# Cross-attention and feed-forward: GpSimd's feed-forward additions in 512-column pieces, the biases on another wait

## The chip, the cores and the metric

The kernel runs on 1 core of one Trainium2 chip. The metric is device time in microseconds (us) of one execution. TensorE (PE in the profile) multiplies, VectorE (DVE), ScalarE (ACT) and GpSimd (POOL) work element by element, SyncE (SP) issues DMAs. The engines run their own instruction lists in order and meet at semaphores.

## The reference, cut to what matters

```python
x = x + xattn(layernorm(x), ctx)          # x: 8 x 1024 x 512, 16 heads, 64 keys
h   = layernorm(x) @ W1 + b1              # 512 -> 2048
im  = w_imag * sin(theta + 0.1 * h)
q   = h + (cos(theta)*w_real + sin(theta)*w_imag) * im * 0.1
x   = x + relu(q) @ W2 + b2               # 2048 -> 512
```

All is float32. The kernel writes every matmul as three, over a high and a low part of each operand (`product`, lines 1983 to 1985), so that splitting into `hi` (ScalarE) and `lo = full - hi` (VectorE) accounts for much of the element work.

## The kernel before, in words

The 8192 rows are 16 tiles of 512 rows (`TILES`), held as 4 blocks (`NB`) of 128 partitions x 512 channels. Up to about 625 us the attention part runs, tile by tile; it is not touched. The rest is the feed-forward part.

Its first two tiles ("the plain part", about 640 to 812 us) go chunk by chunk: 16 chunks of 128 hidden channels for each tile. TensorE makes a chunk of hidden values, ScalarE and VectorE make sin and relu of it, TensorE multiplies it with W2 three chunks later. The other 14 tiles go in pairs, in seven phases T = 1 to 7. In a phase, the first matmul is a Strassen scheme: 8 steps p = 0 to 7, and in each seven products P1, P6, P4, P2, P5, P7, P3 (this order) give four 128 x 512 hidden blocks, two for each tile (i = 8(T-1) + p counts the steps through). After P7, before P3, come the W2 multiplications of two chunks ("seconds") of the pair's first tile. After step 7 come the last two seconds of the first tile and then those of the second tile, c = 0, 1, 2, ...; no new hidden work is made in that stretch, and the operands of the next phase are prepared in it.

What the engines do in a step, in the order of their lists:

- VectorE: `hidden_12` of the step before (L1829), `wave(2)` (L1848), `sum_u` (L1797), `positive_lo` (L1855), `fraction(3)` (L1834), `wave(3)`, `fraction(0)`, then the step's sums `sum_v` (L1805, waits for P7), `hidden_21` (L1814) and `hidden_22` (L1822, the last of them, counts up `c22_done`), then `wave(0)`, in some steps statistics or transposes for later tiles, `fraction(1)`, `fraction(2)`, `positive_lo`, `wave(1)`.
- `fraction` reads frac and turns, `wave` frac and the hidden block, `positive_lo` the hidden block and act_hi: two operands in SBUF each. So do `operand_lo` (L1783), `split_lo` (L1565) and `sum_to_lo` (L1789). The step's sums and `add_outputs` (L1867) have one operand in PSUM; transposes (L1560) and statistics (L1517) have one operand.
- TensorE waits in `strassen`: P5 of the next step for `hidden_12` (`c12_done`), P7 for `sum_u`, P3 for `hidden_22` (`c22_done`); in `second(e)` for `positive_lo` of that chunk, and, where a new output is begun, for `add_outputs` of the output before.
- GpSimd: `add_row_bias` (L904) adds bo to two of the four blocks of a coming tile's rows, `add_last_bias` (L913) adds b2 + bo to two blocks of the residual that the output is added to, `operand_sums` (L1130) makes the Strassen differences T1, T2, T4, T3 of the next phase, one after the other, when `add_outputs` of the first tile is done. `rsqrt` (L881) and `add_parts` (L535, on 256 columns) are smaller.

In a phase before the last, `add_row_bias` is called four times: in step 0 for the first half on P1 and for the second half on P7 of that step, then on P7 of step 1 and on P7 of step 2; `add_last_bias` for the first tile once in step 6 and once in step 7, on their P7. In phase 7 there are only the last biases. The one for the second tile follows `operand_sums` or, in phase 7, follows at once.

```python
for half in range(2):                                   # p = 0 and p = 1
    pool.wait_ge(prod, at_prod(i + (p if half else 0), "P7") - (NP - 2) * (p + half == 0))
    add_row_bias(2 * T + 2 + p, half)
```

Of the kernel before, what the change touches and what calls it, by code (L numbers as in the profile page):

```python
# [11 lines left out]
ALU = mybir.AluOpType  # L12
# [3 lines left out]
P = 128  # L16
BANKS, BANK = 8, 512
B, N, C = 8, 1024, 512
# [10 lines left out]
NB = TOK // P  # L29
# [15 lines left out]
NP = len(PRODUCTS)  # L45
# [107 lines left out]
def xattn_ffn(nc, x, ctxt, wq, bq, wk, bk, wv, bv, wo, bo, w1, b1, phases, w_real, w_imag,  # L153
# [6 lines left out]
    with stack:  # L160
# [32 lines left out]
        bo_row = sbuf(stack, "bo_row", [P, C])  # L193
# [118 lines left out]
        x1_whole = sem("x1_whole")  # L312
# [158 lines left out]
        def at_prod(i, name):  # L471
            return NP * i + PRODUCTS.index(name) + 1
# [389 lines left out]
        def _(pool):  # L862
# [37 lines left out]
            def add_row_bias(T, half):  # L900
                blocks = slice(half * NB // 2, (half + 1) * NB // 2)
                pool.wait_ge(x_in[T % 2], x_loads(TILES + T))
                rows = x_sb[T % 2][:, blocks, :]
                pool.tensor_tensor(rows, rows, bo_row[:].unsqueeze(1).to_broadcast([P, NB // 2, C]), ALU.add)\  # L904
                    .then_inc(x1_whole, 1)

            def add_last_bias(T, half):
                blocks = slice(half * NB // 2, (half + 1) * NB // 2)
                pool.wait_ge(acc_in[T % 2], 16 * (T // 2 + 1))
                if T == 0:  # L910
                    pool.wait_ge(b2_biased, 1)
                rows = acc[:, T % 2, blocks, :]
                pool.tensor_tensor(rows, rows, b2_row[:].unsqueeze(1).to_broadcast([P, NB // 2, C]), ALU.add)\  # L913
                    .then_inc(acc_biased, 1)

            rsqrt(0)

# [200 lines left out]
            def operand_sums(T, names):  # L1118

                for name in names:  # L1120
                    j = OPERAND_SUMS.index(name)
                    if name == "T1":
                        for half in range(2):
                            pool.wait_ge(a_back[half], 16 * (turned_at(2 * T + 1) + 1))
                    else:
                        pool.wait_ge(t_done, 4 * (T - 1) + j)
                    if name == "T4":
                        pool.wait_ge(xo_lo_done, NP * (T - 1) + OPERANDS.index("B21") + 1)
                    a, b = {"T1": ("B12", "B11"), "T2": ("B22", "T1"), "T4": ("T2", "B21"), "T3": ("B22", "B12")}[name]
                    pool.tensor_tensor(PLACE[name], PLACE[a], PLACE[b], ALU.subtract).then_inc(t_done, 1)  # L1130

            for j in range(FC + HALF1 + 4):
                pool.wait_ge(turns_done, j + 1)
# [21 lines left out]
            for T in range(1, FFN_PAIRS):  # L1155
                more = T + 1 < FFN_PAIRS
                for p in range(FP):
                    i = (T - 1) * FP + p
                    if more and p < 2:
                        for half in range(2):  # L1160
                            pool.wait_ge(prod, at_prod(i + (p if half else 0), "P7") - (NP - 2) * (p + half == 0))
                            add_row_bias(2 * T + 2 + p, half)
                    if more and p == 2:
                        rsqrt(TILES + 2 * T + 2)
                    if more and p == 4:
                        rsqrt(TILES + 2 * T + 3)
                    if p >= FP - 2:
                        pool.wait_ge(prod, at_prod(i, "P7"))
                        add_last_bias(2 * T, p - FP + 2)
                if more:  # L1170
                    pool.wait_ge(y2_done, NB * (2 * T + 1))
                    operand_sums(T + 1, OPERAND_SUMS)
                for half in range(2):
                    add_last_bias(2 * T + 1, half)
# [1092 lines left out]
```

## Time and profile before

| | |
|---|---|
| median of 3 runs | 2005.63 us (2000.49 to 2009.94) |
| the profiled execution | 2007.17 us, its span 2005.4 us |
| PE busy | 1957.9 us (98%) |
| VectorE busy | 1605.7 us (80%) |
| ScalarE busy | 1261.5 us (63%) |
| GpSimd busy | 749.9 us (37%) |
| mean granted TensorE clock | 0.995 of full speed |

The span runs from the first to the last instruction; 1.8 us of the execution lie around it. Start times are us from the span's start. In the rows, L is the line of the kernel; in timeline rows the number in square brackets is the time that the engine stood idle before the instruction, and what ended it; "x2" is two instructions merged in one row, with the time from the start of the first to the end of the last. An instruction's recorded time holds also what it waited for after it was issued.

### The profile page before, as it was taken

How to read it: one execution, taken by the hardware profiler on the slowest of the kernel's cores; microseconds unless marked ns; L12 is line 12 of the kernel's file. 1: busy time of each engine (PE TensorE's matmuls, PEld its weight loads, DVE VectorE, ACT ScalarE, POOL GpSimd, SP SyncE). 2: the span in 40 equal slices, each digit the busy share in tenths (PEclk: the TensorE clock that was granted, in tenths of full speed). 3: DMA queues.
4: the chain of work that ended last, by engine and by line, in shares of the span. 5: the costliest groups of instructions: out<-in, count | busy, mean ns of one | idle time of the engine just before them, and what ended most of it. 6: DMA issues, size and time to landing. Idle time of an engine off the chain costs nothing.

```text
span 2005.4 us, 27939 instructions
## 1 busy us (share of the span) xinstructions
PE 1957.9 (98%) x9162; PEld 1625.9 (81%) x9162; DVE 1605.7 (80%) x2272; ACT 1261.5 (63%) x2132; POOL 749.9 (37%) x453
## 2 busy tenths in 40 slices
PE   9999999999999999999999999999999999999999
PEld 7788888888887788787887788788778878878877
DVE  8988888888876987888688778968878886886773
ACT  6767767666655876676477467546736755754661
POOL 6877777777774533202311320311131032031020
PEclk9999999999999999999999999999999999999999
DMA  7465664665536998787778688777877877876645
GB/s 245 149 164 140 171 170 129 174 177 152 157 100 209 315 338 269 263 247 235 263 242 251 223 265 258 244 261 235 237 259 244 253 240 253 257 235 228 225 138 189
DMA packets 347459, 441.29 MB, mean 220 GB/s; under 512 B 165552, under 2 KB 201392, under 8 KB 347312
## 3 DMA queue, kind: packets, MB, share of 16 engines
q1 hardware_dynamic: 346448, 439.44, 70.7%
q8 instruction: 75, 1.23, 0.2%
q14 instruction: 72, 0.59, 0.1%
q10 hardware_dynamic: 864, 0.04, 0.0%
HBM read 347.90 MB, written 91.23 MB: 219 GB/s over the span
## 4 chain that ended last, share of the span: by engine, by line
PE 56%; DVE 22%; ACT 11%; issue 9%; POOL 1%; DVEq 0%; DMA 0%; ACTq 0%; POOLq 0%
PE psum L1983 18%; PE psum L1985 17%; PE psum L1984 17%; DVE frac L1834 4%; ACT turns L1408 3%; DVE act_lo L1855 3%; DVE hid L1848 3%; PE psum L2076 2%; ACT frac L1384 2%; DVE acc L1867 2%; DVE stats L1517 2%; ACT x_sb L1208 2%; ACT act_hi L1436 1%; DVE late_hid L1848 1%; DVE late_hid L1805 1%
## 5 line engine op out<-in xcount | busy, mean ns | idle before, releaser
L1983 PE MATMUL psum<-w_ring,act_hi 128*128 128x512 f32 x1024 | 403.7, 394 | 27.2 <-DVE act_lo L1855 26.1
L1985 PE MATMUL psum<-w_ring,act_lo 128*128 128x512 f32 x1024 | 402.1, 393 | 0.0
L1984 PE MATMUL psum<-w_ring,act_hi 128*128 128x512 f32 x1024 | 402.0, 393 | 0.0
L1983 PE MATMUL psum<-xo,w_ring 128*128 128x512 f32 x784 | 307.6, 392 | 6.0 <-DVE late_hid L1822 3.6
L1985 PE MATMUL psum<-xo,w_ring 128*128 128x512 f32 x784 | 305.8, 390 | 0.0
L1984 PE MATMUL psum<-xo,w_ring 128*128 128x512 f32 x784 | 305.6, 390 | 0.0
L1834 DVE SCALAR_TENSOR_TENSOR frac<-frac,turns 128x512 f32<-128x512 f32 x256 | 223.5, 884 | 68.9 <-ACT frac L1384 68.0
L1983 PEld LDWEIGHTS psum<-w_ring,act_hi 128*128 128x128 f32 x1024 | 194.1, 190 | 73.9 <-issue 33.7
L1421 ACT ACTIVATE frac<-frac 128x512 f32<-128x512 f32 x256 | 156.4, 627 | 151.6 <-DVE frac L1834 151.6
L1985 PEld LDWEIGHTS psum<-w_ring,act_lo 128*128 128x128 f32 x1024 | 194.1, 190 | 40.8
L1984 PEld LDWEIGHTS psum<-w_ring,act_hi 128*128 128x128 f32 x1024 | 194.4, 190 | 40.0
L913 POOL TENSOR_TENSOR acc<-acc,b_row 128x1024 f32<-128x1024 f32 x32 | 85.5, 2684 | 330.6 <-PE psum L1985 330.6
L1384 ACT ACTIVATE frac<-turns,round_col 128x512 f32<-128x512 f32 x256 | 185.3, 724 | 13.4 <-DVE hid L1848 6.2
L904 POOL TENSOR_TENSOR x_sb<-x_sb,bo_row 128x1024 f32<-128x1024 f32 x30 | 76.3, 2552 | 290.0 <-DMA x_sb<-x_dram 150.9
L1983 PEld LDWEIGHTS psum<-xo,w_ring 128*128 128x128 f32 x784 | 147.2, 188 | 46.0 <-issue 15.4
L1985 PEld LDWEIGHTS psum<-xo,w_ring 128*128 128x128 f32 x784 | 147.2, 188 | 30.8
L1984 PEld LDWEIGHTS psum<-xo,w_ring 128*128 128x128 f32 x784 | 147.3, 188 | 29.4
L1436 ACT ACTIVATE act_hi<-late_hid 128x512 fp32r<-128x512 f32 x112 | 70.0, 630 | 158.2 <-PE psum L1985 158.2
L1855 DVE SCALAR_TENSOR_TENSOR act_lo<-late_hid,act_hi 128x512 fp32r<-128x512 f32 x112 | 127.0, 1155 | 42.7 <-ACT act_hi L1436 42.7
L970 POOL TENSOR_TENSOR prob<-prob,top 128x1024 f32<-128x1024 f32 x64 | 122.0, 1906 | 72.8 <-DVE top L1653 72.7
L949 POOL TENSOR_TENSOR prob<-prob,inv 128x1024 f32<-128x1024 f32 x64 | 123.4, 1928 | 42.2 <-DVE inv L1635 42.1
L1848 DVE SCALAR_TENSOR_TENSOR hid<-frac,gain,hid 128x512 f32<-128x512 f32 x134 | 116.3, 868 | 26.9 <-ACT frac L1421 26.9
(187 smaller groups left out, 4420.5 us busy)
## 6 DMA issues: line engine op xcount, KB each, us to landing
w_ring<-w2s SPq DMA_DIRECT2D x240, 512.0 KB, 4.1
w_ring<-w1s SPq DMA_DIRECT2D x392, 256.0 KB, 3.6
x_sb<-turn_dram SPq DMA_DIRECT2D x58, 512.0 KB, 6.0
res<-in_x SPq DMA_DIRECT2D x64, 256.0 KB, 3.6
x_dram<-res SPq DMA_DIRECT2D x64, 256.0 KB, 3.1
acc<-x_dram SPq DMA_DIRECT2D x16, 1024.0 KB, 8.1
x_sb<-in_x SPq DMA_DIRECT2D x15, 1024.0 KB, 6.3
x_sb<-x_dram SPq DMA_DIRECT2D x15, 1024.0 KB, 7.9
```

Of the source, the lines that this page charges most:

```text
L913: pool.tensor_tensor(rows, rows, b2_row[:].unsqueeze(1).to_broadcast([P, NB // 2, C]), ALU.add)\
L949: pool.tensor_tensor(rows, rows, inv[:, (i - 1) % 2, :].unsqueeze(2) .to_broadcast([P, NB * HG, KEYS]), ALU.mult).then_inc(prob_done, 1)
L970: pool.tensor_tensor(rows, rows, top[:, i % 2, :].unsqueeze(2).to_broadcast([P, NB * HG, KEYS]), ALU.subtract).then_inc(shift_done, 1)
L1384: act.activation(frac[:, q % 2, :], turns[:, q % 2, :], ACT.Identity, bias=round_col[:]).then_inc(whole_done, 1)
L1421: act.activation(frac[:, q % 2, :], frac[:, q % 2, :], ACT.Sin, scale=-SIN_SCALE).then_inc(sin_done, 1)
L1436: act.activation(act_hi[:, e % ACTS, :], source, ACT.Relu).then_inc(act_hi_done, 1)
L1834: dve.scalar_tensor_tensor(out=frac[:, q % 2, :], in0=frac[:, q % 2, :], scalar=ROUND, in1=turns[:, q % 2, :], op0=ALU.subtract, op1=ALU.s ...
L1848: dve.scalar_tensor_tensor(out=rows, in0=frac[:, q % 2, :], scalar=gain[:, f:f + 1], in1=rows, op0=ALU.mult, op1=ALU.add).then_inc(wave_do ...
L1855: dve.scalar_tensor_tensor(out=act_lo[:, e % ACTS, :], in0=rows, scalar=0.0, in1=act_hi[:, e % ACTS, :].bitcast(F32), op0=ALU.max, op1=ALU ...
L1983: pe.matmul(o, a_hi, b_hi, start=first, stop=False, skip_group_check=resumed)
L1984: pe.matmul(o, a_hi, b_lo, start=False, stop=False, skip_group_check=resumed)
L1985: return pe.matmul(o, a_lo, b_hi, start=False, stop=last, skip_group_check=resumed)
```

## The change

Three edits, all in GpSimd's list. Both bias helpers go over their two blocks one by one: two additions of 512 columns take the place of one of 1024. Each operand sum is made in two instructions of 512 columns. And the biases of the phases wait for `c22_done` of a step where they waited for one of its products. Only the last piece of each group counts up the semaphore, as the one instruction did. The biases of the plain part keep their place in the list.

```diff
             def add_row_bias(T, half):
                 blocks = slice(half * NB // 2, (half + 1) * NB // 2)
                 pool.wait_ge(x_in[T % 2], x_loads(TILES + T))
-                rows = x_sb[T % 2][:, blocks, :]
-                pool.tensor_tensor(rows, rows, bo_row[:].unsqueeze(1).to_broadcast([P, NB // 2, C]), ALU.add)\
-                    .then_inc(x1_whole, 1)
+                for n in range(blocks.start, blocks.stop):
+                    row = x_sb[T % 2][:, n, :]
+                    last = pool.tensor_tensor(row, row, bo_row[:], ALU.add)
+                last.then_inc(x1_whole, 1)
 
             def add_last_bias(T, half):
...
-                rows = acc[:, T % 2, blocks, :]
-                pool.tensor_tensor(rows, rows, b2_row[:].unsqueeze(1).to_broadcast([P, NB // 2, C]), ALU.add)\
-                    .then_inc(acc_biased, 1)
+                for n in range(blocks.start, blocks.stop):
+                    row = acc[:, T % 2, n, :]
+                    last = pool.tensor_tensor(row, row, b2_row[:], ALU.add)
+                last.then_inc(acc_biased, 1)
...
-                    pool.tensor_tensor(PLACE[name], PLACE[a], PLACE[b], ALU.subtract).then_inc(t_done, 1)
+                    for rows in (slice(0, NB // 2), slice(NB // 2, NB)):
+                        last = pool.tensor_tensor(PLACE[name][:, rows], PLACE[a][:, rows], PLACE[b][:, rows], ALU.subtract)
+                    last.then_inc(t_done, 1)
...
                         for half in range(2):
-                            pool.wait_ge(prod, at_prod(i + (p if half else 0), "P7") - (NP - 2) * (p + half == 0))
+                            pool.wait_ge(c22_done, i + 1 + (p if half else 0))
                             add_row_bias(2 * T + 2 + p, half)
...
                     if p >= FP - 2:
-                        pool.wait_ge(prod, at_prod(i, "P7"))
+                        pool.wait_ge(c22_done, i + 1)
                         add_last_bias(2 * T, p - FP + 2)
```

## Rows read from the trace of the kernel before

**Rows 1.** The page, part 1: busy time and share of the span.
```profile
PE 1957.9 (98%) x9162; PEld 1625.9 (81%) x9162; DVE 1605.7 (80%) x2272; ACT 1261.5 (63%) x2132; POOL 749.9 (37%) x453
```
**Rows 2.** PE's waits: who, for whom, us in total, times, longest.
```profile
PE psum L1983 <- DVE act_lo L1855: 26.1, 14, 2.6
PE psum L1983 <- DVE late_hid L1822: 3.6, 7, 0.6
PE psum L1983 <- ACT p_sb L1391: 1.9, 1, 1.9
PE psum L1983 <- DVE acc L1867: 1.1, 1, 1.1
```
**Rows 3.** PE's timeline: idle times in phases 1, 3 and 7.
```profile
915.22 0.47 PE L1983 MATMUL psum<-xo,w_ring 128*128 128x512 f32 x1 [0.53 <-DVE late_hid L1822]
933.83 0.47 PE L1983 MATMUL psum<-w_ring,act_hi 128*128 128x512 f32 x1 [1.86 <-DVE act_lo L1855]
948.31 0.47 PE L1983 MATMUL psum<-w_ring,act_hi 128*128 128x512 f32 x1 [1.69 <-DVE act_lo L1855]
...
1274.77 0.47 PE L1983 MATMUL psum<-w_ring,act_hi 128*128 128x512 f32 x1 [1.85 <-DVE act_lo L1855]
1287.61 0.47 PE L1983 MATMUL psum<-w_ring,act_hi 128*128 128x512 f32 x1 [1.69 <-DVE act_lo L1855]
...
1951.17 0.47 PE L1983 MATMUL psum<-w_ring,act_hi 128*128 128x512 f32 x1 [2.57 <-DVE act_lo L1855]
```
**Rows 4.** Windows (stretch; length; busy of PE to POOL; clock; DMA), behind idle times.
```profile
933.80:937.20 3.40, 3.37 (x11) 2.71 (x12) 3.15 (x6) 2.69 (x5) 0.00 (x0) 0.69 0.41 160
...
1274.80:1278.20 3.40, 3.40 (x15) 2.83 (x16) 3.15 (x6) 2.63 (x5) 0.00 (x0) 1.00 0.44 171
```
**Rows 5.** By line: duration in ns, min/median/max, of GpSimd's 1024- and 512-column instructions.
```profile
L913 POOL TENSOR_TENSOR acc<-acc,b_row x32: 2388/2838/2959, 696.8 to 1947.1; 128x1024 f32<-128x1024 f32 x32
...
L891 POOL TENSOR_TENSOR q_lo<-q_full,q_hi x61: 1287/1295/1879, 29.2 to 596.6; 128x512 fp32r<-128x512 f32 x61
```
**Rows 6.** GpSimd's timeline: steps 7 of phases 1 and 7, the first operand sum.
```profile
925.09 2.39 POOL L913 TENSOR_TENSOR acc<-acc,b_row 128x1024 f32<-128x1024 f32 x1 [13.35 <-PE psum L1985]
942.05 2.78 POOL L1130 TENSOR_TENSOR temps<-x_sb 128x1024 f32<-128x1024 f32 x1 [14.57 <-DVE acc L1867]
...
1941.88 7.99 POOL L913 TENSOR_TENSOR acc<-acc,b_row 128x1024 f32<-128x1024 f32 x3 [12.55 <-PE psum L1985]
```
**Rows 7.** VectorE's timeline beside GpSimd's 1024- and 256-column instructions in the plain part.
```profile
788.04 2.88 DVE L1848 SCALAR_TENSOR_TENSOR hid<-frac,gain,hid 128x512 f32<-128x512 f32 x1
...
665.04 1.23 DVE L1834 SCALAR_TENSOR_TENSOR frac<-frac,turns 128x512 f32<-128x512 f32 x1
```
**Rows 8.** VectorE's timeline: steps 6 and 7 of phase 1.
```profile
909.41 2.88 DVE L1848 SCALAR_TENSOR_TENSOR late_hid<-frac,gain,late_hid 128x512 f32<-128x512 f32 x1 [0.70 <-ACT frac L1421]
...
925.38 2.66 DVE L1834 SCALAR_TENSOR_TENSOR frac<-frac,turns 128x512 f32<-128x512 f32 x1 [0.58 <-ACT frac L1384]
...
929.52 0.69 DVE L1822 TENSOR_TENSOR late_hid<-psum,late_hid 128x512 f32<-128x512 f32 x1
...
933.00 0.68 DVE L1855 SCALAR_TENSOR_TENSOR act_lo<-hid,act_hi 128x512 fp32r<-128x512 f32 x1
```
**Rows 9.** VectorE's timeline behind phase 1's first output.
```profile
942.49 2.89 DVE L1848 SCALAR_TENSOR_TENSOR late_hid<-frac,gain,late_hid 128x512 f32<-128x512 f32 x1
945.30 3.46 DVE L1855 SCALAR_TENSOR_TENSOR act_lo<-late_hid,act_hi 128x512 fp32r<-128x512 f32 x2
```
**Rows 10.** Timelines, step 0 of phase 1: two GpSimd instructions back to back, VectorE beside them.
```profile
820.33 5.21 POOL L904 TENSOR_TENSOR x_sb<-x_sb,bo_row 128x1024 f32<-128x1024 f32 x2 [21.55 <-DMA x_sb<-x_dram]
...
820.44 2.84 DVE L1848 SCALAR_TENSOR_TENSOR hid<-frac,gain,hid 128x512 f32<-128x512 f32 x1
```
**Rows 11.** Timelines, phase 2: `hidden_12` of step 0, first matmul of step 1's P5.
```profile
996.84 0.68 DVE L1829 TENSOR_TENSOR late_hid<-psum,late_hid 128x512 f32<-128x512 f32 x1
...
1001.47 0.39 PE L1983 MATMUL psum<-xo,w_ring 128*128 128x512 f32 x1
```

## The prediction

> **What bounds the kernel now.** I read the page first: TensorE is busy for 1957.9 of 2005.4 us [rows 1], so a gain can only come from its idle times and its clock. The list of PE's waits names the idle times: 26.1 us in 14 waits for `positive_lo`'s low part (L1855), 3.6 in seven for `hidden_22` (L1822), and one each for ScalarE's P1 copy and for an output sum [rows 2]; all of them lie in the feed-forward part. The timeline of PE then gives their places. A phase has three: A, 0.53 us (P3 of step 6 waits for `hidden_22`); B, 1.86 us behind step 7 (the last seconds wait for `positive_lo`); C, 1.70 us, 14 us later, in the seconds of the second tile [rows 3]. They return in phases 1 to 6 with the same sizes; phase 7 has one B of 2.57 us. The plain part has 1.94 (at 668), 1.07 (at 736) and 1.93 us (at 813), and phase 1 one more of 0.58 at 839.
>
> Five of the idle times are followed by a stretch at the lower clock (1.2 GHz for 2.4): windows behind B read 0.69 in phase 1 and 1.00 in phase 3 [rows 4]. Of six B of 1.86 us three were followed by such a stretch, of six C of 1.70 none, and the 1.94 and the 2.57 were. Its price: from B to C it takes 948.31 - 933.83 = 14.48 us with it and 1287.61 - 1274.77 = 12.84 without [rows 3], so about 1.65 us.
>
> Next, why VectorE is late. Its instructions with two operands in SBUF take about 0.7 us, but 2.66 to 2.9 when a 1024-column GpSimd instruction runs, and end about 0.6 us after that one ends [rows 6 to 9]. Sums with a PSUM operand, transposes and statistics keep their 0.69 us (the `hidden_22` row of [rows 8] is one of them). So GpSimd holds something that the two-operand instructions need, one engine at a time. The Trainium skill ("SBUF — State Buffer", on the two separate sides) says this too: a shared port pair, held for a whole instruction by whichever engine starts first. The trace agrees.
>
> **How long a piece holds it.** Where both engines have work without pause they alternate: in the plain part VectorE's instructions take 2.88 us beside 1024-column ones and 1.23 beside 256-column ones [rows 7]; consecutive ones overlap by about 0.08, so a round is 2.81 and 1.15. With 0.6 us of VectorE's own, the hold is 2.2 us for 1024 columns and 0.55 for 256. A line between them gives 1.1 us for 512. Alone, 512 columns take 1.29 us and 1024 take 2.39 [rows 5], so a pair of pieces is 0.2 us longer than one instruction. The bounds: below, half of 2.2; above, 1.88 us, the longest contested 512-column instruction [rows 5], less the 0.6 it waited, 1.3. I take 1.1. The new operand pattern (a plain row where a repeated one was) is seen in no row at 1024 columns; `q_lo` of [rows 5] has a plain one.
>
> **Does VectorE get in between two pieces?** At 820.33 two GpSimd instructions ran back to back without a wait between them, and VectorE's, issued at 820.44, ended at 823.28, after the first and 2.3 us before the end of the second at 825.54 [rows 10]. So it does. The Trainium skill speaks for a doubt ("GPSIMD Engine Reference", Instruction dispatch): consecutive GpSimd instructions are no barrier, each of the cores begins the next when its own share is done. By that alone a pair of pieces might hold the pair of ports without a gap, and splitting would give nothing; the sum would then be 1997 us, the third rival below, which is worked out from rows. The trace speaks against it here.
>
> **C goes.** When `add_outputs` ends, T1 is issued at 942.05 [rows 6]. Before, `wave(3)` waited for all of it (to 945.38), and the next `positive_lo` for all of T2, to 948.15 [rows 9]; PE had been ready at 946.62. After: piece one holds to 943.6, `wave(3)` ends 944.2, piece two 945.3; act_hi is there at 944.6, so `positive_lo` ends at 945.95, 0.7 before PE needs it. The next has to be done at 946.62 + 2.72 = 949.34 (one second is twelve matmuls at 0.227) and ends about 948.7. Later ones had more slack with holds of 2.2. Six times 1.70: 10.2 us.
>
> **A and B, the moved wait.** Before, the bias of step 6 was issued at P7 and held up `wave` at 909.41 by 2.14 us, the bias of step 7 (925.09) `fraction(0)` at 925.38 by 1.97 [rows 6, 8], both ahead of the step's three sums, which need no shared port. After, nothing holds these; `hidden_22` of step 6 comes about 1.45 us earlier (it is then held by ScalarE's part of the chain), and A is gone. But each bias now meets `wave(0)`, `fraction(1)`, `fraction(2)` and `positive_lo`. In step 7, `hidden_22` ends 1.97 earlier, at 928.24; `wave(0)` goes first, piece one holds 928.85 to 930.0, `fraction(1)` ends 930.6, piece two 931.8, `fraction(2)` 932.45, `positive_lo` 933.05 where it ended 933.68 [rows 8]. So 0.6 us are won of the 2, the rest is given back behind the sums. PE comes 0.53 earlier, since A is gone, while VectorE's chain, late from the bias of step 6, comes only about 0.2 earlier: B is then about 1.55. A and B together: 2.39 less 1.55, 0.85 us, six times 5.1 us. In phase 7 the last three biases are issued together, at 1941.88 before [rows 6], the first hidden wholly by the sums, and two (4.4 us) ahead of `fraction(1)` and `(2)`. After, six pieces from 1944.7 on: three are ahead of `positive_lo`, which ends 1949.8 for 1951.03; B falls to about 1.35, and about 0.5 us come with the pieces behind it. 0.7 us.
>
> **Step 0 to 2.** Both halves of step 0 now stand behind one wait, so four pieces follow each other, from 992.2 in phase 2. They put `wave(0)`, two fractions, `positive_lo` and `wave(1)` 4.4 us apart; `hidden_12` then ends at 999.7 for 997.5, and P5 needs it at 1001.47 [rows 11]: 1.8 us of slack. The delay reaches `fraction(3)` (1.3 us late) and `fraction(0)` of step 1, but that one was held up by a bias before and is no more, so `hidden_22` of step 1 comes at 1009.5, against 1009.73 before and 1009.87 when P3 needs it. Steps 1 and 2: two pieces behind the sums in place of one hold before them, with about 1 us of slack at P5 and P7. Costed at nothing, with this thin cover.
>
> **Plain part.** At 736 a 1024-column hold stands before `add_outputs`; half of it goes: 1.07 us. From 782 to 799 six GpSimd instructions hold VectorE to one instruction in 2.8 us; at 1.7 its backlog (ScalarE's turn at 804.66, which at 5.44 us a chunk was due at 802.2) goes, and with it the 1.93 at 813. At 668 VectorE has work without pause, so the same port time mostly stays: 0.6. At 839 0.3. Together 3.9 us.
>
> **Clock.** All idle times that stay are under 1.70 us, behind which no row has half clock: five stretches of 1.65, 8.2 us.
>
> **Sum.** 10.2 + 5.1 + 0.7 + 3.9 + 8.2 = 28.1 us. The profiled execution took 2007.17 us (span 2005.4), 1.5 more than the median of 2005.63; 2005.6 - 28.1 is 1978 us. No new queue and no DMA is added: the biases issue none, and nothing behind them in GpSimd's list (`rsqrt`, due a step later) is pushed past its time.
>
> **Rivals.**
> 1. The clock does not come back (0.17): B of 1.55 is near 1.70, and what would still be followed by half clock is open. 1978 + 8.2: 1986 us.
> 2. Step 0's four pieces are too many (0.11). If a piece holds 1.6 us rather than 1.1, `hidden_12` comes 0.2 after P5's time and `hidden_22` of step 1 about 1.5 late, six times: 9 us back, 1987. For: the cover of 0.4 at P3. Against: [rows 7].
> 3. No hand-over between pieces (0.08). C, the 736 and the 813 stay, phase 7 gets 2.2 worse, A and B still win 5.1, and three clock stretches go (5.0): 8 us, 1997. Against: [rows 10].
> 4. Slower (0.06): a piece holds the ports nearly as long as 1024 columns did, as if the hold were a cost of the instruction. At 2.2 us, step 0 makes `hidden_22` of step 1 4 us late (24 us in six phases), B grows by 2.2 (13 us) and C stays: about 2043. It decides from about 1.85 us a piece on, where the losses of step 0, B and C (36 us for each us of hold) eat the 28. Against: the 256-column round of 1.15 us.
>
> **Numbers.** My forecast has 0.58. Its own range is 1969 (B gone as well, 9 us more) to 1985. With rivals 1 and 2 that reaches to 1994; rivals 3 and 4 stay outside. 0.5%, 10 us, is about what this measurement tells from no change. Faster: 0.58 + 0.17 + 0.11 = 0.86. Same: rival 3, 0.08. Slower: rival 4, 0.06.
>
> **What would show it.** In the changed profile: no idle PE at C; VectorE's contested instructions at 1.7 to 1.8 us, none at 2.9; `wave` before the sums of steps 6 and 7 at 0.75; B at 1.3 to 1.6 with clock 1.00 behind it; no new wait for `late_hid` in step 1. Wrong, if PE waits there, or if B is above 1.86: then the sums were the better cover.

## The result: 1975.08 us, 1.5% faster, and the profile after

The changed kernel takes 1975.08 us (median of 4 runs, 1974.92 to 1976.86); the kernel before, run beside it, 2005.97 (4 runs, 2000.49 to 2009.94). The ratio is 0.985 (0.9826 to 0.9874). The prediction said 1978 in 1969 to 1994. The profiled execution took 1974.92 us, its span is 1973.1 and its granted clock 1.0; against the span of the profile of before that is 32.3 us less.

The page after, part 1 (to be read beside [rows 1]):
```profile
PE 1944.6 (99%) x9162; PEld 1620.7 (82%) x9162; DVE 1597.4 (81%) x2272; ACT 1264.8 (64%) x2132; POOL 816.8 (41%) x543
```
GpSimd has 90 instructions more and is busier by 67 us (a pair of pieces that takes turns with VectorE is recorded with 3.4 us where the one instruction had 2.39 [rows 6]); TensorE runs the same 9162 matmuls in a span 32 us shorter. Its waits, as in [rows 2]:
```profile
PE psum L1987 <- DVE act_lo L1859: 14.0, 11, 2.0
...
PE psum L1987 <- DVE acc L1871: 0.5, 1, 0.5
...
PE psum L1987 <- ACT p_sb L1395: 0.3, 1, 0.3
```
The lines have moved by four behind the operand sums: L1987 is L1983 of before, L1859 `positive_lo`, L1838 `fraction`, L1852 `wave`, L1826 `hidden_22`. The 26.1 us behind `positive_lo` are 14.0 now, and the wait for `hidden_22` is gone. PE's timeline, the idle times that answer to [rows 3], the one behind step 7 of phases 1, 3 and 6, and phase 7:
```profile
927.27 0.47 PE L1987 MATMUL psum<-w_ring,act_hi 128*128 128x512 f32 x1 [1.70 <-DVE act_lo L1859]
...
1257.85 0.47 PE L1987 MATMUL psum<-w_ring,act_hi 128*128 128x512 f32 x1 [1.58 <-DVE act_lo L1859]
...
1754.19 0.47 PE L1987 MATMUL psum<-w_ring,act_hi 128*128 128x512 f32 x1 [1.86 <-DVE act_lo L1859]
...
1919.04 0.47 PE L1987 MATMUL psum<-w_ring,act_hi 128*128 128x512 f32 x1 [1.40 <-DVE act_lo L1859]
1922.44 0.47 PE L1987 MATMUL psum<-w_ring,act_hi 128*128 128x512 f32 x1 [0.39 <-DVE act_lo L1859]
1925.95 0.47 PE L1987 MATMUL psum<-w_ring,act_hi 128*128 128x512 f32 x1 [0.50 <-DVE acc L1871]
```
A and C are gone from phases 1 to 6, B is there in all six (1.55 to 1.86 us, 9.8 in sum). The windows behind the idle time of 1754, and behind one of 1.98 us at 667.84 in the plain part (columns as in [rows 4]):
```profile
1754.20:1757.60 3.40, 3.40 (x15) 2.84 (x16) 3.14 (x6) 2.58 (x4) 0.00 (x0) 1.00 0.46 181
667.85:671.25 3.40, 3.40 (x15) 2.81 (x16) 3.40 (x6) 2.63 (x5) 0.00 (x0) 1.00 0.52 175
```
The second last number is the DMA share, the one ahead of it the granted clock: 1.00, the level of 2.4 GHz. No stretch at half clock is left in this execution, where the profile of before has six (behind the idle times at 630, 668, 933, 1104, 1443 and 1951).

GpSimd's and VectorE's timelines behind the sums of step 7 of phase 2:
```profile
1087.81 3.44 POOL L915 TENSOR_TENSOR acc<-acc,b_row 128x512 f32<-128x512 f32 x2 [10.82 <-DVE late_hid L1826]
```
```profile
1087.04 0.69 DVE L1826 TENSOR_TENSOR late_hid<-psum,late_hid 128x512 f32<-128x512 f32 x1
1087.64 0.74 DVE L1852 SCALAR_TENSOR_TENSOR hid<-frac,gain,hid 128x512 f32<-128x512 f32 x1
1088.54 3.25 DVE L1838 SCALAR_TENSOR_TENSOR frac<-frac,turns 128x512 f32<-128x512 f32 x2 [0.15 <-ACT frac L1388]
1091.71 0.68 DVE L1859 SCALAR_TENSOR_TENSOR act_lo<-hid,act_hi 128x512 fp32r<-128x512 f32 x1
```
The order is the predicted one: `wave(0)`, piece one, `fraction(1)`, piece two, `fraction(2)`, `positive_lo`. From the end of `hidden_22` to the end of `positive_lo` it takes 1092.39 - 1087.73 = 4.66 us, where the prediction had 4.81. Keep this stretch in mind: it is called the chain below.

### The profile page after: what moved, and what is told of

Read it like the earlier page. It is cut to its first block, busy times and chain, and to the rows that moved or that the text cites. A ratio compares the mean times of both kernels' runs of the same rounds, so it can differ in the third digit from the quotient of the medians.

```text
span 1973.1 us, 28029 instructions
## 1 busy us (share of the span) xinstructions
PE 1944.6 (99%) x9162; PEld 1620.7 (82%) x9162; DVE 1597.4 (81%) x2272; ACT 1264.8 (64%) x2132; POOL 816.8 (41%) x543
## 4 chain that ended last, share of the span: by engine, by line
PE 71%; DVE 14%; ACT 7%; issue 5%; POOL 1%; DMA 0%; DVEq 0%; ACTq 0%; POOLq 0%; SPq 0%
PE psum L1987 23%; PE psum L1989 23%; PE psum L1988 22%; DVE frac L1838 3%; PE psum L2080 3%; ACT turns L1412 2%; DVE act_lo L1859 2%; DVE hid L1852 2%; ACT frac L1388 1%; ACT x_sb L1212 1%; DVE stats L1521 1%; ACT act_hi L1440 1%; DVE temps L1564 1%; DVE late_hid L1809 1%; DVE late_hid L1833 1%
## 5 line engine op out<-in xcount | busy, mean ns | idle before, releaser
L1987 PE MATMUL psum<-w_ring,act_hi 128*128 128x512 f32 x1024 | 399.8, 390 | 14.5 <-DVE act_lo L1859 14.0
L1987 PE MATMUL psum<-xo,w_ring 128*128 128x512 f32 x784 | 305.8, 390 | 0.3 <-ACT p_sb L1395 0.3
L1838 DVE SCALAR_TENSOR_TENSOR frac<-frac,turns 128x512 f32<-128x512 f32 x256 | 220.9, 876 | 65.0 <-ACT frac L1388 64.3
L915 POOL TENSOR_TENSOR acc<-acc,b_row 128x512 f32<-128x512 f32 x64 | 116.8, 1851 | 338.3 <-DVE late_hid L1826 338.3
L1987 PEld LDWEIGHTS psum<-w_ring,act_hi 128*128 128x128 f32 x1024 | 192.2, 188 | 59.6 <-issue 19.9
L1988 PEld LDWEIGHTS psum<-w_ring,act_hi 128*128 128x128 f32 x1024 | 192.3, 188 | 39.5
L905 POOL TENSOR_TENSOR x_sb<-x_sb,bo_row 128x512 f32<-128x512 f32 x60 | 97.3, 1648 | 267.6 <-DVE late_hid L1826 264.8
L1987 PEld LDWEIGHTS psum<-xo,w_ring 128*128 128x128 f32 x784 | 147.2, 188 | 34.3 <-issue 2.9
L1988 PEld LDWEIGHTS psum<-xo,w_ring 128*128 128x128 f32 x784 | 147.2, 188 | 29.9
L1859 DVE SCALAR_TENSOR_TENSOR act_lo<-late_hid,act_hi 128x512 fp32r<-128x512 f32 x112 | 126.7, 1153 | 35.5 <-ACT act_hi L1440 35.5
L1290 ACT ACTIVATE psum<-psum 128x512 f32<-128x512 f32 x128 | 74.5, 583 | 96.1 <-DVE prob L1648 96.1
```

The lines of the kernel that those rows point to most:

```text
L905: last = pool.tensor_tensor(row, row, bo_row[:], ALU.add)
L915: last = pool.tensor_tensor(row, row, b2_row[:], ALU.add)
L1838: dve.scalar_tensor_tensor(out=frac[:, q % 2, :], in0=frac[:, q % 2, :], scalar=ROUND, in1=turns[:, q % 2, :], op0=ALU.subtract, op1=ALU.s ...
L1859: dve.scalar_tensor_tensor(out=act_lo[:, e % ACTS, :], in0=rows, scalar=0.0, in1=act_hi[:, e % ACTS, :].bitcast(F32), op0=ALU.max, op1=ALU ...
L1987: pe.matmul(o, a_hi, b_hi, start=first, stop=False, skip_group_check=resumed)
L1988: pe.matmul(o, a_hi, b_lo, start=False, stop=False, skip_group_check=resumed)
```

## The experiments

Diffs are cuts, against the changed kernel unless said otherwise. Each group ran beside runs of before on one chip, whose medians were 2007.07, 2010.13 and 2004.23; comparisons across groups go by ratios.

**1. The pieces alone: the old waits.**
```diff
-                            pool.wait_ge(c22_done, i + 1 + (p if half else 0))
+                            pool.wait_ge(prod, at_prod(i + (p if half else 0), "P7") - (NP - 2) * (p + half == 0))
...
-                        pool.wait_ge(c22_done, i + 1)
+                        pool.wait_ge(prod, at_prod(i, "P7"))
```


> Additions in 512-column pieces, but the biases wait for P1 and P7 as before the change. My theory (the gain comes from shorter holds of the shared port): C gone, the plain part as in the changed kernel; in step 7 the first piece holds fraction(0) for 1.1 us, the second lies under the sums, so B is 0.9 to 1.2 us; A about 0.3. In total 1972 to 1978 us, the same as the changed kernel within 3 us. Rival (the moved wait brings a good part): A 0.5 and B 1.9 come back, with half clock behind some of them, 1983 us or more.

Measured: 1961.25 us (1960.98 to 1962.93), ratio 0.9779 (0.9761 to 0.9798). The expectation missed, and the interval lies apart from the changed kernel's: moving the waits costs some 14 us of what the pieces alone give. (In the two profiles 1.7 us of this lie at 630 and 668, ahead of the first moved wait, where the two kernels are the same; that part can't come from the move.) Phases 1 to 6 have no A, no B and no C here; one wait for `hidden_22` stands in step 1 of phase 1 (0.57 us at 832). The same stretch as above, GpSimd and VectorE:
```profile
1080.22 2.56 POOL L915 TENSOR_TENSOR acc<-acc,b_row 128x512 f32<-128x512 f32 x2 [12.41 <-PE psum L1989]
```
```profile
1079.22 0.69 DVE L1838 SCALAR_TENSOR_TENSOR frac<-frac,turns 128x512 f32<-128x512 f32 x1 [0.58 <-ACT frac L1388]
1080.18 0.75 DVE L1809 SCALAR_TENSOR_TENSOR late_hid<-psum,par,p_sb 128x512 f32<-128x512 f32 x1 [0.26 <-PE psum L1989]
...
1081.76 0.69 DVE L1826 TENSOR_TENSOR late_hid<-psum,late_hid 128x512 f32<-128x512 f32 x1
1082.36 0.97 DVE L1852 SCALAR_TENSOR_TENSOR hid<-frac,gain,hid 128x512 f32<-128x512 f32 x1
1083.26 0.69 DVE L1838 SCALAR_TENSOR_TENSOR frac<-frac,turns 128x512 f32<-128x512 f32 x1
```
`fraction(0)` has ended (1079.91) before P7 releases the bias at 1080.22; both pieces run at their uncontested 1.29 us beside the three sums, which don't need the port, and end at 1082.78. All that VectorE loses is 0.23 us of `wave(0)` (0.97 for 0.74). In [rows 8] `fraction(0)` came late, behind P7, and was caught. So P7 is the better place as long as VectorE is ahead of it, and the sums are the better cover.

**2. The waits alone: 1024 columns** (before, with the two moved waits).
```diff
-                            pool.wait_ge(prod, at_prod(i + (p if half else 0), "P7") - (NP - 2) * (p + half == 0))
+                            pool.wait_ge(c22_done, i + 1 + (p if half else 0))
...
-                        pool.wait_ge(prod, at_prod(i, "P7"))
+                        pool.wait_ge(c22_done, i + 1)
```


> The waits on c22_done, but 1024 columns in one instruction. Theory of the shorter hold: C (1.70 us in six phases), the 1.07 at 736 and the 1.93 at 813 stay, A is gone, B about 1.5, phase 7's B grows to about 3; 1995 to 2000 us. Rival (the moved wait brings most of it): 1985 us or less.

Measured: 1995.59 us (1991.06 to 1996.6), ratio 0.994 (0.9921 to 0.9959), the time as expected. A goes, C stays, B is 1.43 to 1.78, and phase 7 gets worse, by more than expected (4.66 us where about 3 was). Two idle times of the plain part did not stay as they were, though nothing changes there: the 1.07 at 736 is 0.65 at 740, and in place of the 1.93 at 813 there is 1.84 at 797. PE's idle times in phases 1 and 7:
```profile
931.50 0.47 PE L1983 MATMUL psum<-w_ring,act_hi 128*128 128x512 f32 x1 [1.71 <-DVE act_lo L1855]
944.35 0.47 PE L1983 MATMUL psum<-w_ring,act_hi 128*128 128x512 f32 x1 [1.69 <-DVE act_lo L1855]
...
1939.91 0.76 PE L1983 MATMUL psum<-w_ring,act_hi 128*128 128x512 f32 x1 [4.66 <-DVE act_lo L1855]
```
The moved wait is worth 0.6% with whole instructions and costs 0.7% with pieces: its sign depends on the size of the piece.

**3. The operand sums alone in pieces** (before, with the one edit).
```diff
-                    pool.tensor_tensor(PLACE[name], PLACE[a], PLACE[b], ALU.subtract).then_inc(t_done, 1)
+                    for rows in (slice(0, NB // 2), slice(NB // 2, NB)):
+                        last = pool.tensor_tensor(PLACE[name][:, rows], PLACE[a][:, rows], PLACE[b][:, rows], ALU.subtract)
+                    last.then_inc(t_done, 1)
```


> Only the operand sums in pieces of 512, biases as before the change. Theory: C gone in six phases (10.2 us) and most of the 1.93 at 813; A, B and phase 7's 2.57 stay as they were, with the half-clock stretches behind B: 1991 to 1995 us. Rival (the holds of the sums are only part of C, the VectorE and ScalarE chain is the rest): C keeps 0.5 us or more, 1997 us or more.

Measured: 1989.12 us (1987.81 to 1990.37), ratio 0.9915 (0.9893 to 0.9937), about 2 us better than expected. C is gone in every phase, A (0.51 to 0.53) and B (1.84 to 1.86) stay. So the pieces of the operand sums remove C, without the other edits. The rest of the difference isn't C: only one of the six B, of the same size as in [rows 3], is followed by half clock here, and this profile has two such stretches for six. The 1.93 at 813 did not mostly go, as expected, but stands at 1.58.

**4. The first tile's last biases all but removed.** They add one column of each block in place of 512, so the result lacks the bias in the other columns; instructions and waits stay.
```diff
-            def add_last_bias(T, half):
+            def add_last_bias(T, half, width=C):
...
-                    row = acc[:, T % 2, n, :]
-                    last = pool.tensor_tensor(row, row, b2_row[:], ALU.add)
+                    row = acc[:, T % 2, n, 0:width]
+                    last = pool.tensor_tensor(row, row, b2_row[:, 0:width], ALU.add)
...
-                        add_last_bias(2 * T, p - FP + 2)
+                        add_last_bias(2 * T, p - FP + 2, 1)
```


> The changed kernel, but the first tile's last biases of phases 1 to 7 (steps 6 and 7) add one column of each block instead of 512, so the result lacks the bias in the rest; the instructions and waits stay. Theory: of B's 1.55 us about 1.1 are the two holds, 0.3 to 0.5 stay, 1966 to 1969 us. Rival (B is now VectorE's and ScalarE's own chain, the port has no part in it): B stays above 1.2 us, 1973 us or more.

Measured: 1963.11 us (1962.47 to 1963.54), ratio 0.9786 (0.9765 to 0.9808), 3 us below what was expected. B is gone altogether in phases 1 to 6, where the expectation left 0.3 to 0.5. So without the last biases there is no B. Read alone, this would put the whole price of the moved wait on them.

**5. Each moved wait by itself.** The rows' biases on `c22_done` and the last ones back on P7:
```diff
-                        pool.wait_ge(c22_done, i + 1)
+                        pool.wait_ge(prod, at_prod(i, "P7"))
                         add_last_bias(2 * T, p - FP + 2)
```


> The changed kernel with the first tile's last biases (steps 6 and 7) back on P7; the row biases stay on c22_done. Theory: the 14 us between the changed kernel (1975) and the kernel with pieces and the old waits (1961) come from the last biases ahead of step 7's positive_lo: B gone in phases 1 to 6, 1961 to 1964 us. Rival (the four pieces of step 0 cost most of it): 1969 us or more.

The rows' biases back on P1 and P7, and the last ones on `c22_done`:
```diff
-                            pool.wait_ge(c22_done, i + 1 + (p if half else 0))
+                            pool.wait_ge(prod, at_prod(i + (p if half else 0), "P7") - (NP - 2) * (p + half == 0))
                             add_row_bias(2 * T + 2 + p, half)
```


> The changed kernel with the row biases (steps 0 to 2) back on P1 and P7; the last biases stay on c22_done. Theory: step 0 to 2 have cover, B stays at 1.4 to 1.9, 1972 to 1976 us. Rival (the pieces of step 0 cost most of the 14 us): 1966 us or less.

Measured: 1973.35 us (1970.86 to 1974.9), ratio 0.9828 (0.9801 to 0.9855), and 1966.27 (1965.78 to 1967.56), ratio 0.9789 (0.9763 to 0.9816). Both theories missed, in opposite directions: the theory that the last biases carry the price fell, and its rival, the biases of steps 0 to 2, gets most of it (taking them back wins 0.6% of the 0.7%, taking back the last ones 0.2%, which the intervals hardly tell from nothing). PE's idle times behind step 7, of `last_on_p7` (phases 1 and 3; a wait of 0.51 for `hidden_22`, A, is back too) and of `rows_old` (phases 1 and 3):
```profile
907.61 0.47 PE L1987 MATMUL psum<-xo,w_ring 128*128 128x512 f32 x1 [0.51 <-DVE late_hid L1826]
925.13 0.47 PE L1987 MATMUL psum<-w_ring,act_hi 128*128 128x512 f32 x1 [0.93 <-DVE act_lo L1859]
...
1254.09 0.47 PE L1987 MATMUL psum<-w_ring,act_hi 128*128 128x512 f32 x1 [0.93 <-DVE act_lo L1859]
```
```profile
926.87 0.47 PE L1987 MATMUL psum<-w_ring,act_hi 128*128 128x512 f32 x1 [1.02 <-DVE act_lo L1859]
...
1254.91 0.47 PE L1987 MATMUL psum<-w_ring,act_hi 128*128 128x512 f32 x1 [0.32 <-DVE act_lo L1859]
```
The phases aren't all alike. In `rows_old` phases 2 to 6 have 0.32 or 0.33. In `last_on_p7` five phases have A and B as shown, and phase 2 has neither: there `wave(3)` of step 6 was issued at 1067.16, 0.06 us ahead of GpSimd's piece, and took 0.75 us; in phase 3 it was issued at 1230.67, 0.03 ahead, and took 1.87. A few hundredths of a microsecond decide who is caught.

Yet the rows' biases cause no idle time of PE where they run. That is what the next part is about.

**What joins them: VectorE's lead.** From each timeline I worked out the time from the end of `hidden_22` to the start of P3's first matmul, which waits for it. I call it the lead. The most that it is anywhere is about 2.97 us, when P7 sets the pace and VectorE is fully ahead; at 0.15 P3 starts as soon as the sum is there, and nothing is left. In the changed kernel, step 1 of phase 2, VectorE's and PE's rows:
```profile
998.70 0.69 DVE L1826 TENSOR_TENSOR late_hid<-psum,late_hid 128x512 f32<-128x512 f32 x1
```
```profile
999.54 0.47 PE L1987 MATMUL psum<-xo,w_ring 128*128 128x512 f32 x1
```
999.54 - 999.39 = 0.15. The same for the steps of phase 3 (worked out, us):
```
kernel             step 0    1     2     3     4     5     6     7   | chain  B worked out  B measured
before               2.97  0.15  0.15  1.36  0.73  0.72  0.15  0.14 | 3.48      1.97         1.85
changed              2.97  0.15  0.88  1.36  0.74  0.75  1.03  1.70 | 4.66      1.59         1.58
pieces_old_waits     2.98  1.01  2.72  2.98  2.70  2.67  2.96  2.97 | 3.48      none         none
waits_whole          2.97  0.15  0.95  1.56  0.93  0.91  1.19  1.87 | 4.68      1.44         1.43
last_on_p7           2.97  0.14  0.88  1.36  0.76  0.73  0.15  1.18 | 3.48      0.93         0.93
rows_old             2.97  0.99  2.71  2.97  2.69  2.65  2.94  2.97 | 4.67      0.33         0.32
last_one_column      2.97  0.15  0.87  1.34  0.72  0.71  0.99  2.76 | 3.47      none         none
```
"B worked out" is the chain less the lead at step 7 less 1.37 us. The 1.37 is read from the changed kernel's phase 2, 4.66 - 1.73 - 1.55 = 1.38, and from `rows_old`'s phase 1, 4.68 - 2.29 - 1.02 = 1.37: it is the time that PE's six matmuls from P3's start on are recorded with (1089.46 to 1090.99, 1.53), less the 0.15 between the end of `positive_lo` and the start of the matmul that waits for it. It meets the other rows to 0.01 us, but for a lead of 0.14, where it is 0.12 too much. With phase 7's chain of 5.75 and lead of 2.97 it gives 1.41 for the 1.40 there.

So B has two parts. The last biases behind the sums stretch the chain from 3.48 to 4.67 us. The rows' biases behind the sums of steps 0 to 2 take away the lead (2.72 becomes 0.88 at step 2), and up to step 6 it isn't rebuilt (1.03 for 2.96); why not was not tested. In these steps VectorE itself waits for ScalarE (0.58 us at 1079.22 in experiment 1, and 0.58 at 1084.86 in the changed kernel), so it is the lead of both engines' work. From step 6 to 7 it would come back: without the last biases it is 2.76 at step 7 (`last_one_column`). With the one of step 6 behind the sums it is 1.70, and with that one on P7 1.18. With a full lead the long chain costs 0.33; with the short lead the short chain costs 0.93; in the changed kernel it is 1.59. The lead also fits why P7 was a bad place in the kernel before: with 0.72 at step 5 and 0.15 at step 6 `wave(3)` or `fraction(0)` of the next step comes after P7 and is caught by the bias; with 2.67 and 2.96 they come ahead of it.

**6. Which of the rows' biases.** Last biases on P7 in both. Step 0's rows on the old waits, those of steps 1 and 2 on `c22_done`:
```diff
-                            pool.wait_ge(c22_done, i + 1 + (p if half else 0))
+                            if p:
+                                pool.wait_ge(c22_done, i + 1 + (p if half else 0))
+                            else:
+                                pool.wait_ge(prod, at_prod(i + (p if half else 0), "P7") - (NP - 2) * (p + half == 0))
```


> Pieces, last biases on P7; the row biases of step 0 on P1 and P7 as before the change, those of steps 1 and 2 on c22_done. It splits the 12 us between the two kernels with last biases on P7 (rows on c22_done 1973, rows on products 1961). Theory (VectorE loses its lead over TensorE once, behind the four pieces of step 0, and the equal length of their steps keeps it lost until step 7): the lead at the last sum stays near 1.0 us in step 1 and above 2 us from step 3 on, 1961 to 1965 us. Rival (each bias behind the sums costs by itself, wherever it is): 1967 us or more.

And the other way round (`if not p:`):

> The other half of the split: the row biases of step 0 on c22_done (four pieces in a row), those of steps 1 and 2 on P7. Theory: the lead is 0.15 us in step 1, and partly back in step 3 as in phase 1 of the kernel with the old waits; if the four pieces are what costs, 1967 to 1973 us. Rival (the biases of steps 1 and 2 are what costs): 1961 to 1965 us.

Measured: 1962.08 us (1961.35 to 1963.04), ratio 0.9781 (0.9752 to 0.9809), the time as expected, the leads not (above 2 us from step 3 on was expected); and 1965.78 (1964.82 to 1966.2), ratio 0.9798 (0.9769 to 0.9826), between the ranges of the theory and of its rival: missed. Leads in phase 3: 2.97, 1.43, 2.04, 2.51, 1.85, 1.81, 1.18, 2.94 and 2.98, 0.14, 1.17, 2.26, 1.61, 1.57, 1.18, 2.94. Each half takes part of the lead and leaves at least 1.57 at step 5; both together leave 0.73. With 1.57 or 1.81 `wave(3)` of step 6 comes ahead of the bias on P7, but `fraction(0)` is still caught, which is why step 6 has 1.18; here of `step0_old`:
```profile
1231.06 1.57 DVE L1841 SCALAR_TENSOR_TENSOR frac<-frac,turns 128x512 f32<-128x512 f32 x1 [0.59 <-ACT frac L1391]
```
With 1.18, step 7's comes ahead of P7, and no B is left; both together leave 0.15 at step 6, and `fraction(0)` is caught again. (Phase 1 is an exception: `step0_old` has A and B there, 0.51 and 0.94.) Against experiment 1 the medians are 0.8 and 4.5 us higher, and 12.1 with both at once: the price doesn't look like a sum. The ratios (0.0002, 0.0019 and 0.0049 higher) say the same, but their intervals are wider than these differences; A, B and the new wait named next add up to 1.5 and 3.1 us in the two profiles, and to 7.2 with both. `step0_c22` also shows a new wait of 0.60 to 0.65 us, for `hidden_22` at step 1 of phases 2 to 6; in phase 2 PE, VectorE and GpSimd:
```profile
998.31 0.47 PE L1990 MATMUL psum<-xo,w_ring 128*128 128x512 f32 x1 [0.62 <-DVE late_hid L1829]
```
```profile
994.62 1.37 DVE L1841 SCALAR_TENSOR_TENSOR frac<-frac,turns 128x512 f32<-128x512 f32 x1 [0.34 <-ACT frac L1391]
```
```profile
992.34 3.10 POOL L905 TENSOR_TENSOR x_sb<-x_sb,bo_row 128x512 f32<-128x512 f32 x2 [5.82 <-PE psum L1992]
```
Step 0's four pieces have made VectorE late, so that step 1's, released by P7, catch `fraction(0)` (1.37 us for 0.69) ahead of the sums.

**7. Smaller pieces** of 256 columns, with the old waits (the same in `add_last_bias`).
```diff
-                    row = x_sb[T % 2][:, n, :]
-                    last = pool.tensor_tensor(row, row, bo_row[:], ALU.add)
+                    for cols in (slice(0, C // 2), slice(C // 2, C)):
+                        row = x_sb[T % 2][:, n, cols]
+                        last = pool.tensor_tensor(row, row, bo_row[:, cols], ALU.add)
...
-                    for rows in (slice(0, NB // 2), slice(NB // 2, NB)):
+                    for rows in (slice(n, n + 1) for n in range(NB)):
```


> Old waits, all additions of the change in pieces of 256 columns. If the hold goes by columns (0.55 us a piece), no VectorE instruction of 512 columns beside them takes over 1.25 us and the time is that of the 512-column pieces or a little less: 1958 to 1962 us. If a piece has a fixed part in its hold (rival 4 of the prediction), VectorE's contested instructions stay near 1.5 us and twice as many turns of the port make it slower: 1964 us or more.

Measured: 1962.74 us (1960.73 to 1964.41), ratio 0.9772 (0.9745 to 0.98): not to be told from 512 columns, and 0.7 us above the range expected for a hold by columns. VectorE beside eight pieces back to back, and one of those stretches on GpSimd:
```profile
659.19 1.22 DVE L1854 SCALAR_TENSOR_TENSOR hid<-frac,gain,hid 128x512 f32<-128x512 f32 x1
660.34 1.23 DVE L1840 SCALAR_TENSOR_TENSOR frac<-frac,turns 128x512 f32<-128x512 f32 x1
```
```profile
654.15 8.72 POOL L906 TENSOR_TENSOR x_sb<-x_sb,bo_row 128x256 f32<-128x256 f32 x8
```
The round is 1.15 us, so the hold goes by columns (rival 4 falls), and VectorE gets a turn between any two of eight consecutive GpSimd instructions. In this execution, what it wins in the phases it gives back in the plain part, in a longer stop with half clock (0.50):
```profile
672.67 0.76 PE L1989 MATMUL psum<-w_ring,act_hi 128*128 128x512 f32 x1 [3.40 <-DVE act_lo L1861]
```
```profile
672.70:676.10 3.40, 3.40 (x8) 2.72 (x9) 3.40 (x6) 2.83 (x7) 0.00 (x0) 0.50 0.62 207
```

**8. A better version.** The old waits, and the first tile's last biases in steps 3 and 5 in place of 6 and 7, so that phase 7 ends with two pieces fewer at a time.
```diff
-                    if p >= FP - 2:
-                        pool.wait_ge(c22_done, i + 1)
-                        add_last_bias(2 * T, p - FP + 2)
+                    if p in (3, 5):
+                        pool.wait_ge(prod, at_prod(i, "P7"))
+                        add_last_bias(2 * T, (p - 3) // 2)
```


> Pieces of 512, old waits, but the first tile's last biases in steps 3 and 5 on P7 (they were in 6 and 7). Theory: phases 1 to 6 unchanged (no idle time to win there), phase 7's idle time of 1.63 us goes, since the second tile's biases follow in step 5 and 6: 1959 to 1961 us. Rival (the biases in steps 3 and 5 beside the transposes bring new waits for late_hid): 1964 us or more.

Then the stop in the plain part as well, by a later second half of tile 2's bias:
```diff
-                if j in (4, 5):
-                    add_row_bias(2, j - 4)
+                if j in (4, 6):
+                    add_row_bias(2, (j - 4) // 2)
```


> Pieces of 512 and old waits, the first tile's last biases in steps 3 and 5 on P7, and in the plain part the second bias of tile 2 one chunk later (j = 6 for 5), so that it does not meet the sums of a weight pair. Theory: the idle time at 667 (1.3 to 2.0 us, once followed by half clock) falls below 1 us: 1957 to 1959 us. Rival (VectorE has work without pause there, the same port time stays): 1960 us or more.

Measured: 1959.93 us (1958.26 to 1961.07), ratio 0.9756 (0.9729 to 0.9782), as expected, the lowest of all, though its interval overlaps that of experiment 1; and 1961.41 (1959.43 to 1961.77), ratio 0.9774 (0.9746 to 0.9803), a miss, as its rival had it. In `early_p7` phase 7's idle times are gone. In both, one stop of more than 1 us is left in the feed-forward part behind 640, here of the first and of the second; for comparison experiment 1, whose plain part is that of `early_p7`:
```profile
667.06 0.47 PE L1987 MATMUL psum<-w_ring,act_hi 128*128 128x512 f32 x1 [1.96 <-DVE act_lo L1859]
```
```profile
673.53 0.47 PE L1987 MATMUL psum<-w_ring,act_hi 128*128 128x512 f32 x1 [1.92 <-DVE act_lo L1859]
```
```profile
665.41 0.47 PE L1987 MATMUL psum<-w_ring,act_hi 128*128 128x512 f32 x1 [1.29 <-DVE act_lo L1859]
```
The third row is a warning. Eight of the kernels here have the same plain part; six profiles show 1.26 to 1.29 us at this place, and 0.27 to 0.29 six us later, the changed kernel and `early_p7` 1.98 and 1.96. So the 1.92 of `best`, read once, doesn't tell what moving the bias does to the stop; only the time says that it wins nothing.

## Why the prediction was right, and where it was not

**The mechanism and C: right.** One instruction at a time, 0.6 us of VectorE's own, a hold by columns. VectorE's row behind phase 1's first output, for [rows 9]:
```profile
934.27 1.78 DVE L1852 SCALAR_TENSOR_TENSOR late_hid<-frac,gain,late_hid 128x512 f32<-128x512 f32 x1
```
1.78 for 2.89, as forecast. GpSimd's pieces, duration in ns, min/median/max, of the changed kernel (and, second fence, of 256 columns):
```profile
L915 POOL TENSOR_TENSOR acc<-acc,b_row x64: 1719/1743/2283, 696.2 to 1921.7; 128x512 f32<-128x512 f32 x64
```
```profile
L1135 POOL TENSOR_TENSOR temps<-x_sb x28: 737/1182/1195, 780.1 to 1752.7; 128x256 f32<-128x256 f32 x28
```
The rounds are 2.81, about 1.70 and 1.15 us, less 0.6 a hold of 2.2, 1.1 and 0.55. Of VectorE's SCALAR_TENSOR_TENSOR instructions without a PSUM operand, behind 800 us, 63 took over 1.9 us before and none does now. Rivals 3 and 4 have fallen. The doubt that the Trainium skill gives cause for ("GPSIMD Engine Reference", Instruction dispatch: the next GpSimd instruction may begin before all cores have ended the last) is not borne out for the ports: in no kernel with all additions in pieces of 512 did such an instruction take over 1.9 us there, so VectorE got in between back-to-back pieces. C went, shown by experiments 2 and 3.

**The sum, term by term** (profiled executions):
```
term             predicted   measured   how
C                   10.2       10.5     five of 1.70 and one of 2.04 gone
A and B              5.1        4.4     A, six of 0.47 to 0.53, gone; B 11.1 to 9.8
phase 7              0.7        0.3     2.57 to 1.40 + 0.39 + 0.50
plain part           3.9        3.0     736: 1.07 to 0.23; 813: 1.93 to 0.29; 839: 0.58 to 0; 668: 1.94 to 1.98
at 630                 -        0.7     2.71 to 2.01, a wait for ScalarE
new                    -       -0.4     0.25 at 632, 0.16 at 660
clock                8.2        9.9     six stretches at 1.65; the sixth, at 630, wasn't counted
stops' hidden part     -        1.5     9 stops fewer at 0.16
```
They make 29.9 of 32.3 us; 2.4 stay open, partly waits too short to be shown. The prediction read all six C as 1.70; the one of phase 4 is longer, and the clock behind it is full:
```profile
1458.36 0.47 PE L1983 MATMUL psum<-w_ring,act_hi 128*128 128x512 f32 x1 [2.04 <-DVE act_lo L1855]
```
At 813 the idle time now stands at 809.35, for the same ScalarE copy. The terms of the plain part are less sure than they look, since its idle times differ from execution to execution: where nothing had changed yet, experiments 2 and 3 have 0.65 and 0.70 for the 1.07 at 736. At 668 the 0.6 were worth nothing in this profile; in the six others with the same plain part the stop is 1.3 us, as the term has it, with 0.3 six us later.

**The step that failed is "A and B, the moved wait", with "Step 0 to 2" behind it.** Its numbers for the changed kernel hold (chain 4.81 predicted and 4.66 measured, B 1.55 predicted and 1.55 to 1.86 measured, no new wait in step 1). What failed is what it credited to the move: it took the rows of before, where the bias on P7 caught `wave` and `fraction(0)`, and carried that loss into a kernel with pieces, although pieces alone already remove it (experiment 1). So it saw a gain of 0.85 us a phase from the move, where against the pieces alone the move brings back a whole B. And it costed steps 0 to 2 at nothing because no idle time of PE stood there. The cost was there all the same, as lead, and fell due at step 7: 0.86 us of lead less at step 1 and 1.84 less at step 2 stop no matmul, yet are the reserve that would have hidden most of the longer chain (0.33 in `rows_old`). The test that it named, "if B above 1.86: then the sums were the better cover", was the wrong one: B came at 1.55, and the sums were still the better cover. The total came out because the sum was made for the two edits together, and for them its B was right; what each is worth it had wrong. The pieces alone give 2.2%, more than the whole sum of 1.4%, and the move takes 0.7% of it back.

**Rival 1, the clock:** it came back fully, in all four runs (0.999 and 1.0). That the term was right is in part luck. It rested on all idle times that stay being under 1.70 us, and three were clearly above: 2.01 at 630, 1.98 at 667, and B of phase 6 with 1.86. Whether their size has a part in it is not shown: idle times of 1.98 and 1.86 us in the changed kernel were followed by full clock, those of 1.96 and 1.92 in experiment 8 by windows at 0.58 and 0.68. **Rival 2** had the right place and the wrong form: four pieces in step 0 cost nothing at P5 or P3 of the changed kernel, and take lead.

## What to carry to other kernels

When two engines take turns at a port, as VectorE and GpSimd do here, make the longer holder's instructions short first, and only then ask where they should start: the best place for a whole instruction was not the best place for two halves. An edit costs nothing only if it leaves the lead of the engine ahead of the bottleneck as it was; read the lead step by step (end of the producer to start of its consumer), since a loss in one step is paid where the lead next runs out, and two edits that cost little one by one can be dear together (0.8 and 4.5 us, and 12.1). Measure each part alone: the whole was 1.5% faster here, and one of its parts was 0.7% of loss. And before a single stop is read as the work of an edit, look at it in other profiles of the same code: the one at 668 had two sizes, 1.3 and 2.0 us.

## What the runs showed of the hardware that was not expected

Half clock behind an idle time of 1.84 to 2.05 us came in some executions and not in others, at the same place: in the plain part behind 1.98 us the window read 1.00, behind 1.96 it read 0.58; at C of phase 4 it read 1.00 behind 2.04 in the profile of before and 0.50 behind 2.05 in experiment 2's. The six B of 1.84 to 1.86 us were followed by it three times in the profile of before and once in experiment 3's. The runs of before spread over 10 us, those of the changed kernel over 2. The record puts this spread down to the clock: the runs of before at 2000.7 to 2001.0 us have a mean granted clock of 0.998, those at 2008.1 to 2010.5 of 0.993 or 0.994, and 0.004 to 0.005 of 2005 us are 8 to 10 us.

A stop costs about 0.16 us more than the idle time in the profile's row: a matmul is recorded with 0.39 us, but the next one normally starts 0.227 after its start.

With VectorE's stops gone, another wait shows, of 0.32 and 0.57 us, twice in experiment 1's span: W2's loads into the weight ring. PE's row there:
```profile
1440.99 0.50 PE L1987 MATMUL psum<-w_ring,act_hi 128*128 128x512 f32 x1 [0.32 <-DMA w_ring<-w2s]
```
